# Softmax of two attentions: maxima subtracted by VectorE, one exponential of 512 columns in place of four with a bias

## Chip, core and metric

The kernel runs on one core of a Trainium2 chip. The metric is the device time of one execution in microseconds. Engines are named as in the profile: PE is TensorE (PEld its weight loads), DVE is VectorE, ACT is ScalarE, POOL is GpSimd, SP is SyncE.

## What is computed

A chain of layers on 16 sequences of 128 tokens and 256 channels. Two of them, the second layer's "ffn" (phase l1f) and the fourth layer's cross attention (phase l3x), hold a softmax attention of 16 heads of 16 channels, and both go through the same helper in the kernel. Cut to what matters:

```python
def _L1_ffn_ref(x, W_gate, W_qkv):            # phase l1f
    gating = jax.nn.softmax(x @ W_gate.T, axis=-1)
    ...
    att = jnp.einsum('bhqd,bkd->bhqk', q, k_shared) * (1.0 / math.sqrt(hd))
    att = jnp.where(causal[None, None, :, :], att, -jnp.inf)
    att = jax.nn.softmax(att, axis=-1)
    y = jnp.einsum('bhqk,bkd->bhqd', att, v_shared)
    ...
def _L3_xattn_ref(x, cond, mask, ...):        # phase l3x
    q = _w8a8_linear(x, wq, bq).reshape(B, N, H, D).transpose(0, 2, 1, 3)
    ...
    scores = jnp.einsum('bhnd,bhld->bhnl', q, k) * inv_sqrt_d + mask[:, None]
    attn = jax.nn.softmax(scores, axis=-1)
    o = jnp.einsum('bhnl,bhld->bhnd', attn, v)
    ...
    return _w8a8_linear(o, wo, bo)
```

Each row of each head's 128x128 scores has its maximum taken off, is put through exp, multiplied with the values and divided by its sum.

## The kernel before

The program is a sequence of phases with a barrier behind each. Every phase treats the 16 sequences ("blocks") one after the other, in a software pipeline. The list `order` gives the steps of a turn with their lags: in turn t, step (name, lag) works on block t - lag. Every engine walks the same list and does its own part of each step, so the list is also the order in each engine's queue. In phase l1f:

```python
order = (("S0", 2), ("P3", 3), ("stats", 0), ("V2", 3), ("qkv", 1),
         ("S1", 2), ("P0", 2), ("V3", 3), ("oT", 3), ("pick", 1), ("rows", 1),
         ("S2", 2), ("P1", 2), ("V0", 2), ("turn", 1), ("back", 3), ("normalise", 0), ("ternary", 0),
         ("S3", 2), ("P2", 2), ("V1", 2), ("xT", 0), ("divide", 3))
```

Class `HeadSoftmax` does the 16 heads in four groups of four heads, s = 0 to 3; a group's scores fill one PSUM bank, 128x512 f32. There are two banks `pS`, two tiles `ex` for the exponentials, two tiles `exT` for the transposed ones, and one bank `pP` for the transposes.

- Step S of group s. PE: `scores`, a matmul that writes the mask and one that adds q times k. DVE: `maximum` (line 1226), the negated maximum of each of the four heads, `negmax`. ACT: `exp` (line 1201), four activations of 128 columns each, with the head's `negmax` as bias.
- Step P. PE: `turn` (line 1167), four transposes of `ex` into `pP`. Then the evacuation of `pP` to `exT`: by ACT for groups 0 and 3 (line 1220), by DVE for groups 1 and 2 (line 1232).
- Step V. PE: `values` (line 1175), four matmuls with the values into `pO`. After the fourth group ACT copies `pO` to `oT` (line 1209), PE turns it back, and DVE divides by the sums (lines 1246, 1248).

What is interleaved differs. In l1f DVE also has "pick" (lines 1348 to 1354) and "rows" (lines 1358 to 1367, it makes the queries, the shared key `k_rows` and the values of the next block), the layer norm (`stats` lines 150 and 152, `xn` line 167) and a "ternary" step on weights of a later phase (lines 556 to 561). PE has "qkv" (line 895), the transposes "turn" of queries and keys (lines 866, 869), which ACT copies out (lines 877, 883), and "xT" (line 178, copied out by ACT in line 184). In l3x DVE quantises x and the attention's output (lines 1611 to 1626); PE turns the quantised x ("xq", line 1468), ACT copies it out (xqT, line 1509) and then copies the last two strips of kT ("spread", line 883); PE's next S0 waits for these. Its mask is f32 and comes by DMA.

`after(engine, semaphore, v)` waits until the semaphore has reached v, and is left out where v is a constant that is not positive. `hold` waits and then increments a spare semaphore, so that the instruction behind it starts only when the wait is met.

Of the kernel before, what the change touches and what calls it, by code (L numbers as in the profile page):

```python
# [13 lines left out]
ALU = mybir.AluOpType  # L14
ACT = mybir.ActivationFunctionType
AX = mybir.AxisListType
# [5 lines left out]
B, P, C = 16, 128, 256  # L22
# [8 lines left out]
def bc(ap, n):  # L31

    return ap.unsqueeze(2).to_broadcast([ap.shape[0], ap.shape[1], n])
# [6 lines left out]
class Chain:  # L40


    def __init__(self, eng, sem, per):
        self.eng, self.sem, self.per, self.base, self.n = eng, sem, per, None, per
# [42 lines left out]
def hold(eng, sem, v, spare):  # L87

    eng.wait_ge(sem, v)
    eng.sem_inc(spare, 1)  # L90


def after(eng, sem, v):

    if not (isinstance(v, int) and v <= 0):
        eng.wait_ge(sem, v)
# [802 lines left out]
def phase_l1_attention(nc, D, G):  # L899
# [7 lines left out]
    with Phase(nc, "l1x") as ph:  # L907
# [64 lines left out]
        def _(pe):  # L972
# [58 lines left out]
            for s in range(4):  # L1031
                steps[f"S{s}"] = lambda b, p, s=s: scores(b, p, s)
                steps[f"V{s}"] = lambda b, p, s=s: values(b, p, s)
            pipeline(pe, order, steps, peel=6)

        @block.scalar
        def _(act):
            def exp(b, p, s):
                act.wait_ge(clipped, 4 * b + s + 1)
                after(act, pv_done, 4 * b + s - 1)  # L1040
                act.activation(ex[s % 2][:].rearrange("p m t -> p (m t)"), sc[s % 2][:],
                               ACT.Exp).then_inc(exp_done, 1)

            def turn_out(b, p):
                act.wait_ge(attT_ps, b + 1)
                after(act, out_ps, b)
                act.activation(attT[:].rearrange("p k t -> p (k t)"), pT[:, C:2 * C],
                               ACT.Copy).then_inc(attT_ready, 1)

            def o_turned(b, p):  # L1050
                act.wait_ge(pv_done, 4 * b + 4)
                after(act, back_ps, b)
                act.activation(oT[:], pO[:], ACT.Copy).then_inc(oT_ready, 1)

            steps = {"xT": lambda b, p: nm.scalar(act, b, p), "turn": lambda b, p: tq.scalar(act, b, p),
                     "spread": lambda b, p: tq.scalar_rest(act, b, p), "attT": turn_out, "oT": o_turned}
            for s in range(4):
                steps[f"S{s}"] = lambda b, p, s=s: exp(b, p, s)
            pipeline(act, order, steps, peel=6)
# [73 lines left out]
class HeadSoftmax:  # L1133
# [7 lines left out]
    def __init__(self, ph, G, tq, pS, pP, pO, pB, mask_id, mask_of, v_of, k_of):  # L1141
        self.G, self.tq, self.pS, self.pP, self.pO, self.pB = G, tq, pS, pP, pO, pB
        self.mask_id, self.mask_of, self.v_of, self.k_of = mask_id, mask_of, v_of, k_of
        (self.sc_ps, self.max_ready, self.exp_done, self.pT_ps, self.pT_ready, self.pv_done, self.oT_ready, self.back_ps,
         self.norm_steps, self.normalised) = (
            ph.sem(n) for n in ("sc_ps", "max_ready", "exp_done", "pT_ps", "pT_ready", "pv_done", "oT_ready", "back_ps",
                                "norm_steps", "normalised"))
        self.oT = ph.sb("oT", [P, 4 * P])
        self.negmax = [ph.sb(f"negmax{i}", [P, 4]) for i in range(2)]
        self.ex = [ph.sb(f"ex{i}", [P, 4, P]) for i in range(2)]  # L1150
        self.exT = [ph.sb(f"exT{i}", [P, 4, P]) for i in range(2)]
        self.rec = ph.sb("rec", [P, NH])

    def scores(self, pe, b, p, s):
        if s == 0:
            pe.wait_ge(self.tq.ready, b + 1)
        after(pe, self.exp_done, 4 * b + s - 1)
        bank = self.pS[s % 2]
        pe.matmul(bank[:], lhsT=self.mask_id[:], rhs=self.mask_of(p), start=True, stop=True)
        pe.matmul(bank[:], lhsT=self.tq.plain[p][:, s, :], rhs=self.k_of(p, s).rearrange("p h t -> p (h t)"),  # L1160
                  start=False, stop=True, skip_group_check=True).then_inc(self.sc_ps, 1)
# [33 lines left out]
        return steps  # L1195

    def exp(self, act, b, p, s):
        act.wait_ge(self.max_ready, 4 * b + s + 1)
        after(act, self.pT_ps, 4 * b + s - 1)
        for m in range(4):  # L1200
            ins = act.activation(self.ex[s % 2][:, m, :], self.pS[s % 2][:, m * P:(m + 1) * P], ACT.Exp,  # L1201
                                 bias=self.negmax[s % 2][:, m:m + 1])
        ins.then_inc(self.exp_done, 1)

    def o_turned(self, act, b):

# [15 lines left out]

    def maximum(self, dve, b, p, s):
        dve.wait_ge(self.sc_ps, 4 * b + s + 1)
        after(dve, self.exp_done, 4 * b + s - 1)
        dve.tensor_reduce(self.negmax[s % 2][:], self.pS[s % 2][:].rearrange("p (m t) -> p m t", m=4), AX.X,  # L1226
                          ALU.max, negate=True).then_inc(self.max_ready, 1)

    def evacuate(self, dve, b, p, s):
        dve.wait_ge(self.pT_ps, 4 * b + s + 1)  # L1230
# [399 lines left out]
def phase_l2_attention(nc, D, G):  # L1630
# [12 lines left out]
    with Phase(nc, "l2x") as ph:  # L1643
# [67 lines left out]
        def _(pe):  # L1711
# [87 lines left out]

            def slot(b, p, g, last):  # L1800
                scores(b, p, g)
                if at_least(b, g, 1):
                    turn_probs(*before(b, p, g, 1))
# [705 lines left out]
```

## Time and profile before

| | us |
|---|---|
| median of 3 runs | 3066.3 |
| lowest and highest | 3066.07, 3066.52 |
| the profiled execution | 3068.69 |
| its span, first to last instruction | 3066.9 |
| phase l1f, first S0 to its end | about 1128 to 1376 of the span |
| phase l3x | about 2355 to 2640 of the span |

The profile is one execution. Its page gives the busy time of each engine; a windows view gives the same for chosen stretches, with the granted clock of PE (1.00 is full speed); a timeline lists the instructions in order of time, with the idle time of their engine before them and what ended it. An instruction's duration is not what it costs its engine: neighbours on one engine overlap where they do not depend on each other.

### The profile page before, as it was taken

The numbers are of one execution on the slowest core, as the hardware profiler recorded it, in microseconds if no ns is written. First come the engines' busy times: TensorE is split into PE (matmuls) and PEld (weight loads), VectorE is DVE, ScalarE is ACT, GpSimd is POOL, SyncE is SP. The second block draws the span as 40 slices with busy tenths as digits, with TensorE's granted clock in tenths as the row PEclk, the third lists the DMA queues.
The fourth block names the chain that finished last, engine by engine and source line by source line (L and its number), as shares of the span: only waits on it lengthen the run. The fifth ranks groups of instructions, "written<-read, shape, count | busy, mean of one in ns | idle before, by whom it ended". The sixth has DMA issues, their size and how long they took to land. (4 is left out here: it accounts for less than half of the span.)

```text
span 3066.9 us, 38953 instructions
## 1 busy us (share of the span) xinstructions
PE 2516.7 (82%) x11114; PEld 1545.9 (50%) x11141; DVE 1472.6 (48%) x3480; ACT 1064.3 (35%) x3193; POOL 583.8 (19%) x888
## 2 busy tenths in 40 slices
PE   2476799999978868878999999996444888689998
PEld 1223477667745534434666666664222554446665
DVE  3496311111135557765666666665775666521111
ACT  1002122222225535544555555553222555311111
POOL 1242122222212310003333333331000000101110
PEclk9996899999989979999999999998666999689999
DMA  2400000000030000000000000002000000000000
GB/s 78 186 0 1 8 6 8 5 5 5 5 124 1 0 2 1 0 6 1 1 0 0 0 0 0 0 0 98 0 0 3 4 3 4 0 1 0 0 0 27
DMA packets 20673, 44.76 MB, mean 15 GB/s; under 512 B 3712, under 2 KB 16384, under 8 KB 19200
## 3 DMA queue, kind: packets, MB, share of 16 engines
q1 hardware_dynamic: 20608, 43.98, 4.0%
q8 instruction: 31, 0.51, 0.1%
q14 instruction: 34, 0.28, 0.0%
HBM read 41.87 MB, written 2.10 MB: 14 GB/s over the span
## 5 line engine op out<-in xcount | busy, mean ns | idle before, releaser
L717 DVE TENSOR_TENSOR moe_hid<-moe_act_g,moe_pU 128x384 f32<-128x384 f32 x128 | 70.9, 554 | 444.2 <-ACT moe_act_g L689 444.2
L689 ACT ACTIVATE moe_act_g<-moe_pG 128x384 f32<-128x384 f32 x128 | 62.8, 490 | 425.3 <-PE moe_pU L644 425.3
L644 PE MATMUL moe_pG<-big,moe_xT 128*128 128x384 f32 x512 | 187.5, 489 | 4.1 <-POOL moe_xT L611 4.1
L1867 ACT ACTIVATE l2x_prob<-l2x_pS,l2x_nb,l2x_rms_q 128x256 f32<-128x256 f32 x256 | 142.4, 565 | 133.3 <-DVE l2x_nb L2015 133.3
L623 POOL TENSOR_TENSOR moe_hidw<-moe_hid,moe_data_w_all 128x384 f32<-128x384 f32 x128 | 105.8, 826 | 427.4 <-DVE moe_hid L717 420.7
L644 PE MATMUL moe_pU<-big,moe_xT 128*128 128x384 f32 x512 | 187.1, 488 | 0.0
L665 PE MATMUL moe_pO<-big,moe_hT 128*128 128x256 f32 x768 | 186.8, 380 | 0.0
L895 PE MATMUL l2x_pQ<-big,l2x_xT 128*128 128x512 f32 x320 | 154.6, 606 | 13.6 <-POOL l2x_cT L1944 10.9
L665 PEld LDWEIGHTS moe_pO<-big,moe_hT 128*128 128x128 f32 x768 | 136.0, 190 | 13.2
L689 ACT ACTIVATE l3f_act_g<-l3f_pG 128x512 f32<-128x512 f32 x64 | 38.2, 597 | 286.9 <-PE l3f_pU L644 286.9
L2012 DVE TENSOR_REDUCE l2x_negmax<-l2x_pS 128x2 f32<-128x512 f32 x128 | 87.7, 685 | 98.3 <-PE l2x_pS L1756 95.4
L644 PE MATMUL l3f_pG<-big,l3f_xT 128*128 128x512 f32 x256 | 122.2, 600 | 12.7 <-POOL l3f_xT L611 12.7
L644 PEld LDWEIGHTS moe_pU<-big,moe_xT 128*128 128x128 f32 x512 | 97.9, 191 | 68.5 <-issue 1.2
L1756 PE MATMUL l2x_pS<-l2x_kT,l2x_qT 128*128 128x256 f32 x512 | 128.3, 380 | 0.0
L1848 ACT ACTIVATE l2x_square<-l2x_pQ 128x128 f32<-128x128 f32 x384 | 101.7, 292 | 62.4 <-PE l2x_pQ L895 62.4
L1776 PE MATMUL l2x_pT<-big,l2x_oT 128*128 128x256 f32 x512 | 121.1, 379 | 0.7 <-ACT l2x_oT L1875 0.7
L644 PE MATMUL l3f_pU<-big,l3f_xT 128*128 128x512 f32 x256 | 121.5, 597 | 0.0
L644 PEld LDWEIGHTS moe_pG<-big,moe_xT 128*128 128x128 f32 x512 | 97.7, 191 | 46.2 <-issue 5.9
L665 PE MATMUL l3f_pO<-big,l3f_hT 128*128 128x256 f32 x512 | 120.9, 379 | 0.0
L1767 PE MATMUL l2x_pOT<-l2x_probT,l2x_v 128*128 128x512 f32 x256 | 120.4, 592 | 0.0
L1776 PEld LDWEIGHTS l2x_pT<-big,l2x_oT 128*128 128x128 f32 x512 | 97.0, 190 | 40.2 <-issue 28.7
L1201 ACT ACTIVATE l3x_ex<-l3x_pS,l3x_negmax 128x128 f32<-128x128 f32 x256 | 73.0, 368 | 127.1 <-DVE l3x_negmax L1226 122.2
(421 smaller groups left out, 5309.6 us busy)
## 6 DMA issues: line engine op xcount, KB each, us to landing
big<-in_e_gate SPq DMA_DIRECT2D x1, 3072.0 KB, 10.5
big<-in_e_up SPq DMA_DIRECT2D x1, 3072.0 KB, 17.4
big<-in_e_down SPq DMA_DIRECT2D x1, 3072.0 KB, 24.3
moe_lanes<-in_l2f_lanes SPq DMA_DIRECT2D x16, 192.0 KB, 2.8
x_all<-in_x SPq DMA_DIRECT2D x1, 2048.0 KB, 8.1
hyA_ctx<-in_ctx SPq DMA_DIRECT2D x16, 128.0 KB, 2.0
hyena_toep_rev<-in_k_rev SPq DMA_DIRECT2D x1, 2048.0 KB, 8.4
big<-in_l_wq SPq DMA_DIRECT2D x1, 2048.0 KB, 7.7
```

The source lines that it names most:

```text
L623: pool.tensor_tensor(hidw[c % 2][:].rearrange("p (e i) -> p e i", e=n), hid[c % 2][:].rearrange("p (e i) -> p e i", e=n), bc(w, chunk // n ...
L644: last = pe.matmul(ps[:, 0:chunk], lhsT=xT[p][:, k, :], rhs=w(k, c), start=(k == 0), stop=(k == KC - 1))
L665: last = pe.matmul(pO[p][:, 0:C], lhsT=hT[c % 2][:, k, :], rhs=w_down(c * KT + k), start=(c == 0 and k == 0), stop=(c == NC - 1 and k == K ...
L689: act.activation(act_g[c % 2][:], pG[c % 2][:, 0:chunk], ACT.Silu).then_inc(silu_done, 1)
L895: last = pe.matmul(out, lhsT=xT[:, k, :], rhs=w[:, k, cols], start=(k == 0), stop=(k == KC - 1))
L1201: ins = act.activation(self.ex[s % 2][:, m, :], self.pS[s % 2][:, m * P:(m + 1) * P], ACT.Exp, bias=self.negmax[s % 2][:, m:m + 1])
L1756: last = pe.matmul(pS[j][:, h * 2 * P:(h + 1) * 2 * P], lhsT=qT[g % 2][:, 2 * j + h, :], rhs=kT[p][:, g, :, :].rearrange("p a k -> p (a k) ...
L1767: last = pe.matmul(pOT[:], lhsT=v[p][:, a, g * P:(g + 1) * P], rhs=probT[:, a, :, :].rearrange("p h t -> p (h t)"), start=(a == 0), stop=( ...
L1776: last = pe.matmul(pT[:, C:2 * C], lhsT=oT[:, h, :], rhs=W["l2_wo"][:, 4 * g + h, :], start=(h == 0), stop=(h == 3))
L1848: ins = act.activation(square[u % 2][:, h, :], pQ[:, h * P:(h + 1) * P], ACT.Square, accum_out=ssq[u % 2][:, h:h + 1])
L1867: ins = act.activation(prob[g % 2][:, h, :], pS[j][:, (h % 2) * 2 * P:(h % 2 + 1) * 2 * P], ACT.Exp, scale=rms_q[g][:, h:h + 1], bias=nb[: ...
L2012: dve.tensor_reduce(negmax[:, c], pS[j][:].rearrange("p (h k) -> p h k", h=2), AX.X, ALU.max, negate=True).then_inc(S["max_steps"], 1)
```

## The change

DVE takes the maximum without negating it (`top`), waits until PE has transposed what stood in the tile `ex` two groups before, waits for its own reduce, and subtracts the broadcast maxima from the bank in one tensor_tensor of 128x512, writing to `ex` in SBUF. A new semaphore `shifted` tells of it. ACT then takes one exponential of all 512 columns, in place in `ex`, with no bias. PE's scores, which overwrite a bank, wait for the subtraction of two groups before in place of the exponential.

```diff
-        self.negmax = [ph.sb(f"negmax{i}", [P, 4]) for i in range(2)]
+        self.shifted = ph.sem("shifted")
+        self.top = [ph.sb(f"top{i}", [P, 4]) for i in range(2)]
...
     def scores(self, pe, b, p, s):
...
-        after(pe, self.exp_done, 4 * b + s - 1)
+        after(pe, self.shifted, 4 * b + s - 1)
...
     def exp(self, act, b, p, s):
-        act.wait_ge(self.max_ready, 4 * b + s + 1)
-        after(act, self.pT_ps, 4 * b + s - 1)
-        for m in range(4):
-            ins = act.activation(self.ex[s % 2][:, m, :], self.pS[s % 2][:, m * P:(m + 1) * P], ACT.Exp,
-                                 bias=self.negmax[s % 2][:, m:m + 1])
-        ins.then_inc(self.exp_done, 1)
+        act.wait_ge(self.shifted, 4 * b + s + 1)
+        flat = self.ex[s % 2][:].rearrange("p m t -> p (m t)")
+        act.activation(flat, flat, ACT.Exp).then_inc(self.exp_done, 1)
...
     def maximum(self, dve, b, p, s):
         dve.wait_ge(self.sc_ps, 4 * b + s + 1)
-        after(dve, self.exp_done, 4 * b + s - 1)
-        dve.tensor_reduce(self.negmax[s % 2][:], self.pS[s % 2][:].rearrange("p (m t) -> p m t", m=4), AX.X,
-                          ALU.max, negate=True).then_inc(self.max_ready, 1)
+        scores = self.pS[s % 2][:].rearrange("p (m t) -> p m t", m=4)
+        dve.tensor_reduce(self.top[s % 2][:], scores, AX.X, ALU.max).then_inc(self.max_ready, 1)
+        after(dve, self.pT_ps, 4 * b + s - 1)
+        hold(dve, self.max_ready, 4 * b + s + 1, self.G["spare"])
+        dve.tensor_tensor(self.ex[s % 2][:], scores, bc(self.top[s % 2][:], P), ALU.subtract).then_inc(self.shifted, 1)
```

On DVE in phase l1f, from the end of "rows" over the step S of group 2 to the layer norm (`vs` holds the values, `xn` the normalised x; - before, + with the change):

```order
 L1364 TENSOR_TENSOR l1f_picked<-l1f_pV,l1f_val 128x256
 L1367 TENSOR_REDUCE l1f_vs<-l1f_picked 128x16
-L1226 TENSOR_REDUCE l1f_negmax<-l1f_pS 128x4
+L1224 TENSOR_REDUCE l1f_top<-l1f_pS 128x4
+L1227 TENSOR_TENSOR l1f_ex<-l1f_pS,l1f_top 128x512
 L1232 COPY l1f_exT<-l1f_pP 128x512
 L167 TENSOR_SCALAR l1f_xn<-x_all,l1f_ln_mv,l1f_ln_rstd 128x256
```

The subtraction stands between the reduce and the evacuation of P1; nothing else changes place.

On ACT in phase l3x, from the step "aq" (the quantised attention output) to "spread", over the exponential of group 3:

```order
 L1514 ACTIVATE l3x_aqT<-l3x_pT 128x256
 L877 ACTIVATE l3x_qT<-l3x_pTq 128x512
 L883 ACTIVATE l3x_kT<-l3x_pTk 32x4x128 x2
-L1201 ACTIVATE l3x_ex<-l3x_pS,l3x_negmax 128x128 x4
+L1201 ACTIVATE l3x_ex<-l3x_ex 128x512
 L1509 ACTIVATE l3x_xqT<-l3x_pT 128x256
 L883 ACTIVATE l3x_kT<-l3x_pTk 32x4x128 x2
```

Four activations become one, and the order stays. On DVE in phase l3x, around the step S of group 3, between the quantised x (`qx_q`) and the division of an earlier block (`rec`, `att`), in a turn ahead of the loop:

```order
 L1621 TENSOR_SCALAR l3x_qx_y<-l3x_xn,l3x_qx_inv 128x256
 L1626 TENSOR_SCALAR l3x_qx_q<-l3x_qx_y 128x256
-L1226 TENSOR_REDUCE l3x_negmax<-l3x_pS 128x4
+L1224 TENSOR_REDUCE l3x_top<-l3x_pS 128x4
+L1227 TENSOR_TENSOR l3x_ex<-l3x_pS,l3x_top 128x512
 L1232 COPY l3x_exT<-l3x_pP 128x512
 L1246 RECIPROCAL l3x_rec<-l3x_pQK 128x16
 L1248 TENSOR_TENSOR l3x_att<-l3x_pQK,l3x_rec 128x256
```

Here too one instruction comes in behind the reduce.

## Rows read from the trace of the kernel before

**Rows 1.** The page's head and first section: busy us, share, instructions.
```profile
span 3066.9 us, 38953 instructions
PE 2516.7 (82%) x11114; PEld 1545.9 (50%) x11141; DVE 1472.6 (48%) x3480; ACT 1064.3 (35%) x3193; POOL 583.8 (19%) x888
```

**Rows 2.** Windows of one block each, two of l1f, one of l3x; first the columns.
```profile
core 0: us, PE busy (x) PEld busy (x) DVE busy (x) ACT busy (x) POOL busy (x), PEclk, DMA share, GB/s
1243.20:1258.05 14.85, 13.03 (x81) 6.67 (x80) 10.96 (x29) 7.95 (x27) 0.74 (x2) 1.00 0.00 0
1258.05:1272.78 14.73, 12.66 (x79) 6.74 (x80) 10.88 (x30) 7.96 (x27) 0.74 (x2) 1.00 0.00 0
2481.99:2498.94 16.95, 14.82 (x94) 8.55 (x93) 11.87 (x31) 9.24 (x26) 1.21 (x3) 1.00 0.01 4
```

**Rows 3.** Waits in the l1f block from 1243.20: who for whom, us, times, longest.
```profile
ACT l1f_ex L1201 <- DVE l1f_negmax L1226: 6.9, 4, 2.6
DVE l1f_negmax L1226 <- PE l1f_pS L1160: 2.6, 1, 2.6
```

**Rows 4.** Timeline of l1f, start and duration in us, in brackets idle time before.
```profile
1255.26 0.17 DVE L1342 TENSOR_REDUCE l1f_one<-l1f_pV 128x1 f32<-128x16 f32 x1 [0.25 <-PE l1f_pV L895]
...
1258.05 0.69 DVE L1226 TENSOR_REDUCE l1f_negmax<-l1f_pS 128x4 f32<-128x512 f32 x1 [2.62 <-PE l1f_pS L1160]
...
1262.02 0.65 PE L866 MATMUL l1f_pTq<-ident,l1f_q_rows 128*128 128x128 f32 x4 [0.48 <-DVE l1f_k_rows L1362]
...
1262.83 0.68 DVE L1226 TENSOR_REDUCE l1f_negmax<-l1f_pS 128x4 f32<-128x512 f32 x1
...
1263.43 0.68 DVE L1232 COPY l1f_exT<-l1f_pP 128x512 f32<-128x512 f32 x1
...
1265.91 0.68 DVE L1226 TENSOR_REDUCE l1f_negmax<-l1f_pS 128x4 f32<-128x512 f32 x1
...
1266.62 1.14 ACT L1201 ACTIVATE l1f_ex<-l1f_pS,l1f_negmax 128x128 f32<-128x128 f32 x4 [0.51 <-DVE l1f_negmax L1226]
...
1267.82 0.66 PE L1167 MATMUL l1f_pP<-ident,l1f_ex 128*128 128x128 f32 x4
...
1272.78 0.69 DVE L1226 TENSOR_REDUCE l1f_negmax<-l1f_pS 128x4 f32<-128x512 f32 x1 [2.62 <-PE l1f_pS L1160]
```

**Rows 5.** Groups of instructions kept apart by shape, busy us and mean ns; one timeline row.
```profile
L717 DVE TENSOR_TENSOR l3f_hid<-l3f_act_g,l3f_pU 128x512 f32<-128x512 f32 x32 | 22.0, 687 | 155.5 <-ACT l3f_act_g L689 155.5
L1226 DVE TENSOR_REDUCE l1f_negmax<-l1f_pS 128x4 f32<-128x512 f32 x64 | 43.8, 685 | 49.2 <-PE l1f_pS L1160 48.4 <-issue 0.6
L559 DVE TENSOR_SCALAR l1f_ternary_tmp<-l1f_ternary_tmp 128x384 f32<-128x384 f32 x16 | 5.8, 359 | 0.6
L1041 ACT ACTIVATE l1x_ex<-l1x_sc 128x512 f32<-128x512 f32 x64 | 40.3, 630 | 86.3 <-DVE l1x_sc L1095 59.8 <-PE l1x_pO L1004 25.8
L689 ACT ACTIVATE l3f_act_g<-l3f_pG 128x512 f32<-128x512 f32 x64 | 38.2, 597 | 286.9 <-PE l3f_pU L644 286.9
...
1269.55 0.18 DVE L152 BATCH_NORM_AGGREGATE l1f_ln_mv<-l1f_ln_stats 128x2 f32<-128x6 f32 x1 [0.16 <-DVE l1f_ln_stats L150]
```

**Rows 6.** Timeline of l3x, one block.
```profile
2485.69 0.69 DVE L1226 TENSOR_REDUCE l3x_negmax<-l3x_pS 128x4 f32<-128x512 f32 x1 [0.83 <-PE l3x_pS L1160]
...
2489.26 0.69 DVE L1226 TENSOR_REDUCE l3x_negmax<-l3x_pS 128x4 f32<-128x512 f32 x1 [0.77 <-PE l3x_pS L1160]
...
2493.36 0.69 DVE L1226 TENSOR_REDUCE l3x_negmax<-l3x_pS 128x4 f32<-128x512 f32 x1 [0.85 <-PE l3x_pS L1160]
...
2494.08 1.14 ACT L1201 ACTIVATE l3x_ex<-l3x_pS,l3x_negmax 128x128 f32<-128x128 f32 x4 [1.17 <-DVE l3x_negmax L1226]
...
2495.09 0.40 ACT L1509 ACTIVATE l3x_xqT<-l3x_pT 128x256 bf16<-128x256 bf16 x1
...
2495.64 0.38 PE L895 MATMUL l3x_pT<-l3x_woT,l3x_aqT 128*128 128x256 bf16 x2 [1.31 <-ACT l3x_xqT L1509]
...
2496.84 1.12 PE L1159 MATMUL l3x_pS<-l3x_mask,ident 128*128 128x512 f32 x2 [0.82 <-ACT l3x_kT L883]
```

**Rows 7.** Windows of two later blocks of l3x, columns as in rows 2.
```profile
2498.94:2517.80 18.86, 16.62 (x93) 9.18 (x92) 12.06 (x30) 9.24 (x26) 1.09 (x3) 0.88 0.01 3
2517.80:2537.57 19.77, 17.64 (x95) 9.83 (x94) 11.88 (x31) 9.24 (x26) 1.22 (x3) 0.86 0.01 3
```

## The prediction

> **What bounds the kernel now.** I start with the page [rows 1]: PE is busy 82% of the span, DVE 48%, ACT 35%. By those shares DVE has plenty of room, but they are averages over nine phases, and the change touches only two, l1f and l3x. So next come the windows, one block of each phase at a time [rows 2]. A block of l1f takes 14.85 or 14.73 us, PE busy 12.66 to 13.03, DVE 10.9, ACT 8.0. A block of l3x takes 16.95 us, PE 14.82, DVE 11.87, ACT 9.24. In neither is an engine full; what sets the period is a loop of dependences, to be followed in the timeline.
>
> In **l1f** [rows 4] the loop reads: DVE's reduce of S1 starts at 1258.05, that of S2 at 1262.83, that of S3 at 1265.91. Between them DVE carries no idle time: pick, rows, the evacuation of P1, xn and the ternary step stand there back to back (the list of waits of a block names DVE only before S1 [rows 3]). The exponential of S3 starts at 1266.62, and PE's P3 at 1267.82, as that ends. Then PE works through V2, the projections (qkv) and the scores of S1 without a gap until DVE can start the next S1 at 1272.78. The pieces: 7.86 us of DVE in a row, 1.91 from the reduce of S3 to P3, 4.96 of PE: 14.73, the period. DVE's only long idle stretch, 2.6 us a block [rows 3, 4], lies in the PE part of the loop, before S1. So in l1f each DVE microsecond between S1 and S3 is on the path though DVE is 74% busy; ACT is on it once a block, with the exponential of S3.
>
> In **l3x** [rows 6] DVE waits for PE's scores before each reduce (0.83, 0.77 and 0.85 us before S1, S2 and S3), while PE runs without a gap up to the transposes of x. There the loop leaves PE: reduce of S3 at 2493.36, exponential at 2494.08, then in ACT's order xqT at 2495.09 and the last two strips of kT, and PE's next S0 at 2496.84. PE waits 1.31 us for the first and 0.82 us for the second. So the path holds one reduce and one exponential a block.
>
> **The change part by part.** *The new subtraction.* A tensor_tensor of 128x512 f32 with one operand in PSUM stands in the trace: 687 ns [rows 5]. The broadcast of four maxima over 128 columns is the only difference. I take 0.69 us. It depends on the reduce just ahead of it; the same construction (a wait on DVE's own semaphore, held by an increment) in the statistics leaves 0.16 us idle, where independent neighbours overlap: S2's reduce to the copy behind it is 0.60 us from start to start at a duration of 0.68 [rows 4, 5]. So one group costs DVE 0.69 + 0.15 = 0.84 us more from start to start, 3.4 us a block, 64 groups in each phase. Bounds: below, 0.45 + 0.03 = 0.48, if it ran at the rate of the tensor_scalar from SBUF (359 ns for 384 columns [rows 5], 0.45 for 512) and the wait cost as little as 0.03; above, 1.0, with twice the wait. I take 0.84, since the row of the same instruction is the nearest.
>
> *The exponential.* Four of 128 columns take 1.14 us together [rows 4], one of 512 from SBUF to SBUF in l1x 630 ns [rows 5]: 0.51 us less, in each of 128 groups. Reading SBUF instead of the bank costs ACT something: 597 ns is the row with a PSUM source [rows 5], 33 ns apart.
> The Trainium skill (page "VectorE: DVE Perf Modes", section on the TRN2 errata) gives ScalarE a larger fixed cost for an SBUF source than for PSUM, 224 against 172 cycles; an estimate from these is 43 ns. That speaks against the change, the trace agrees in size, and by the page's figure the sum below would be about 0.3 us longer (29 exponentials on the path, 10 ns each).
>
> *The step from scores to finished exponential.* Before, on S3 of l1f: 1.91 us from the reduce to P3 [rows 4]. After: 0.69 + 0.15 + 0.69 + 0.03 + 0.63 + 0.06 = 2.25. So **+0.33 us** where DVE has waited for scores; where groups queue up on DVE, +0.84 for each.
>
> *The bank.* PE's scores wait for the subtraction two groups back instead of the exponential. PE's own order has the transposes of that group ahead, and they wait for its exponential, so this wait is met already, before and after: 0. Likewise DVE's new wait for the transposes of group s-2 (their tile is overwritten): PE did them before the scores that DVE has just waited for: 0. Behind the subtraction on DVE are queued the pick and rows chain (S1), the evacuation of P1 (S2) and P2 (S3), and PE's turn, P2 and P3 wait for these.
>
> *Sum for l1f.* S1 and S2 lengthen DVE's stretch by 0.84 each, and S3's step grows by 0.33: +2.01 us a block. Everything else on the loop's way I shift by the same rows: PE's turn, already waiting 0.48 for k_rows [rows 4], comes 0.84 later, P2 some 1.2 later, xT some 1.2 later, and P3 2.0 later. It is P3 that closes the loop, as before. P2's evacuation on DVE ends about when the exponential of S3 does, at no extra cost. DVE's own work is then 14.73 - 2.62 - 0.25 (its wait for pV) + 3.36 = 15.2 us [rows 4], under the new period of 16.75: it idles 1.5 before S1. There are 16 blocks (64 reduces, four a block [rows 5]), 14 periods from the S1 of the first to that of the fifteenth: 28.1. In the last two blocks DVE waits for scores again; up to 8 steps of 0.33 there: 2.6. **l1f: +30.7 us.**
>
> *Sum for l3x.* The exponential of S3 starts 0.84 later, and xqT behind it starts 0.53 after it instead of 1.01 (one instruction less its overlap with the next): +0.36 a block on both PE waits, 15 periods: 5.4. DVE's slack of 0.77 to 0.85 before S1 to S3 is just used up by 0.84 each; what is missing, under 0.1 in every second block, gives 0.7. The tail, where PE waits for single exponentials, about 3 times 0.33: 1. **l3x: +7.1 us.** The cover here is thin: each further 0.1 us of a subtraction would put about 0.2 a block on the path, 3 us in all.
>
> Nothing else moves: the other phases run the same instructions, and POOL and SP have no part in the groups. The profiled execution took 3068.69 (span 3066.9), the median is 3066.3; the difference of 37.8 goes onto the median. **Forecast: 3066.3 + 30.7 + 7.1 = 3104.1, so 3104 us.**
>
> **Rivals.** *A, the clock falls more often (14%).* In l3x PE waits twice within 2.6 us each block, and in two blocks running the granted clock was 0.88 and 0.86 instead of 1.00, so part of them ran at 1.2 in place of 2.4 GHz; they took 18.86 and 19.77 us against some 17.0 [rows 2, 7], 2.3 us more each. The change stretches these waits to 1.67 and 0.85, and in l1f puts waits of near 1 us before the turn and P3, with PE's share down from 86% to 77%. Against it: l1f shows 1.00 in the blocks of [rows 2] with waits of 0.5 us, and l3x mostly 1.00 with 1.31. If five more blocks fall: +12, 3116; if every one of the 15 periods did: 13 more at 2.3, +30, 3134.
> [...]
>
> *B, the subtraction is cheap (5%).* At the lower bound of 0.45 us with a 0.15 wait, l1f gains 2 x 0.60 + 0.09 a block, 18 us plus 1 in the tail, and l3x about 2: 3087. Against it: both f32 tensor_tensor rows run at one column per ns.
>
> *C, DVE's idle time hides it (4%).* DVE idles 3.9 us a block in l1f, and the four groups need 3.4. Were these idle pieces spread between S1 and S3, only the latency of +0.33 in l3x would remain: 3072, within 0.2%. The timeline speaks against it, since 2.62 of the 3.9 lie in one piece behind PE.
>
> *D, faster (3%).* Were ACT's queue what PE waits for, the shorter exponential would pay: in l3x 0.48 a block on xqT, in l1f 0.51 on P3, together 15 x 0.48 + 16 x 0.51 = 15.4, so 3051. PE's waits do name ACT (1.31, 0.82). It needs the subtraction to cost nothing on the path: it decides below 0.48 us from start to start in l3x, and below 0.17 in l1f (0.51 over three groups). The nearest row says 0.84.
>
> **How the numbers follow.** My forecast holds 72% (3097 to 3112, with the self-wait between 0.05 and 0.25 us and the two slow blocks there or gone, -4.7), A 14%, B 5%, C 4%, D 3%; 2% is for what I have not seen. From 3091 to 3121 takes the forecast, the first half of A and the upper edge of B: 8 in 10 or somewhat more. 0.2% is 6 us, about what a measurement of this kernel can tell from no change. Slower by more than that: forecast, A, B and part of the rest, 0.94; within it: C, 0.03; faster: D, 0.03.
>
> **What would show each step.** In the profile after: the subtraction at 0.69 with 0.15 idle before it, the exponential at 0.63; a block of l1f at 16.75 with DVE without a gap from S1 to S3, P3 released by ACT or DVE, and DVE's wait before S1 down from 2.62 to 1.5; a block of l3x at 17.3 with DVE's waits before S1 to S3 near 0, and PE's wait for xqT at 1.67. I am wrong if the l1f block stays below 16, if l3x grows by more than 1 us a block at a clock of 1.00, or if the clock rows fall in l1f.

## The result and the profile after

The changed kernel takes 3136.0 us (3133.9 to 3137.9 over four runs), the kernel before beside it on the same chip 3066.4. The ratio is 1.0226, 95% interval 1.0209 to 1.0244: slower by 69.6 us. I had forecast 3104, in a range from 3091 to 3121. The direction was right; the size lies outside the range.

The page's head and first section, changed kernel (busy us, share of the span, instructions; compare [rows 1]):

```profile
span 3136.1 us, 38599 instructions
PE 2553.2 (81%) x11114; PEld 1564.9 (50%) x11141; DVE 1559.3 (50%) x3608; ACT 1005.7 (32%) x2809; POOL 585.4 (19%) x888
```

DVE has 86.7 us more, for 128 new instructions, ACT 58.6 less, as meant. But PE, whose instructions are the same in number (11114), is busy 36.5 us longer. The same work took PE longer, and the granted clock is where to look.

The two new instructions by form, busy us and mean ns, then idle time before them:

```profile
L1227 DVE TENSOR_TENSOR l1f_ex<-l1f_pS,l1f_top 128x512 f32<-128x512 f32 x64 | 44.3, 692 | 9.1
L1201 ACT ACTIVATE l1f_ex<-l1f_ex 128x512 f32<-128x512 f32 x64 | 40.3, 630 | 167.9 <-DVE l1f_ex L1227 167.9
```

**l1f.** Two blocks, windows from S1 to S1, then the waits of the first of them (columns as in [rows 2, 3]):

```profile
core 0: us, PE busy (x) PEld busy (x) DVE busy (x) ACT busy (x) POOL busy (x), PEclk, DMA share, GB/s
1290.83:1307.74 16.91, 13.00 (x81) 6.67 (x80) 13.68 (x33) 6.06 (x15) 0.74 (x2) 1.00 0.00 0
1307.74:1324.46 16.72, 12.60 (x79) 6.74 (x80) 13.57 (x33) 6.06 (x15) 0.74 (x2) 1.00 0.00 0
```

```profile
ACT l1f_ex L1201 <- DVE l1f_ex L1227: 10.7, 4, 3.9
DVE l1f_top L1224 <- PE l1f_pS L1161: 1.6, 1, 1.6
```

The timeline of that block, cut to the loop (start, duration, in brackets idle time before), answers to [rows 4]:

```profile
1290.83 0.69 DVE L1224 TENSOR_REDUCE l1f_top<-l1f_pS 128x4 f32<-128x512 f32 x1 [1.59 <-PE l1f_pS L1161]
1291.66 0.69 DVE L1227 TENSOR_TENSOR l1f_ex<-l1f_pS,l1f_top 128x512 f32<-128x512 f32 x1
1292.27 0.16 DVE L1348 TENSOR_REDUCE l1f_val<-l1f_g 128x1 f32<-128x16 f32 x1
...
1300.27 0.68 DVE L1224 TENSOR_REDUCE l1f_top<-l1f_pS 128x4 f32<-128x512 f32 x1
1301.10 0.69 DVE L1227 TENSOR_TENSOR l1f_ex<-l1f_pS,l1f_top 128x512 f32<-128x512 f32 x1
...
1301.82 0.63 ACT L1201 ACTIVATE l1f_ex<-l1f_ex 128x512 f32<-128x512 f32 x1 [1.81 <-DVE l1f_ex L1227]
...
1302.79 0.66 PE L1168 MATMUL l1f_pP<-ident,l1f_ex 128*128 128x128 f32 x4 [0.92 <-ACT l1f_ex L1201]
...
1307.74 0.69 DVE L1224 TENSOR_REDUCE l1f_top<-l1f_pS 128x4 f32<-128x512 f32 x1 [1.72 <-PE l1f_pS L1161]
```

This is the picture that was forecast. The subtraction starts 0.83 us after its reduce. From the reduce of S1 to that of S3 it is 9.44 us in place of 7.86, from there to P3 2.52 (2.26 in the next block) in place of 1.91, and PE's part up to the next S1 is 4.95, as before. DVE's idle time before S1 shrank from 2.62 to 1.59. Fourteen periods grew from 206.4 to 234.6 us, and the phase ended 31.3 us later (1369.2 to 1400.5; the table of times before puts its end too late, at about 1376).

**l3x.** Five blocks in a row, windows from S0 to S0; compare 16.95 at a clock of 1.00 in [rows 2] and the two of [rows 7]:

```profile
2514.33:2534.68 20.35, 17.65 (x94) 9.78 (x93) 14.75 (x35) 7.46 (x14) 1.09 (x3) 0.84 0.01 3
2534.68:2554.58 19.90, 17.31 (x94) 9.75 (x93) 14.57 (x34) 7.46 (x14) 1.22 (x3) 0.86 0.01 3
2554.58:2572.96 18.38, 15.68 (x94) 8.78 (x93) 14.66 (x35) 7.46 (x14) 1.09 (x3) 0.95 0.01 4
2572.96:2592.90 19.94, 17.35 (x94) 9.55 (x93) 14.56 (x34) 7.46 (x14) 1.22 (x3) 0.84 0.01 3
2592.90:2613.22 20.32, 17.61 (x94) 9.76 (x93) 14.75 (x34) 7.46 (x14) 1.09 (x3) 0.84 0.01 3
```

None of the 15 blocks runs at full clock; before, 12 of 15 did. The same matmuls keep PE busy 15.7 us in one block of four and 17.3 to 17.7 in the others, where it was 14.8. The 15 periods from the first S0 to the sixteenth grew from 258.0 to 292.8 us. The timeline of one block shows where in it the clock goes; it answers to [rows 6]:

```profile
2547.22 0.69 DVE L1224 TENSOR_REDUCE l3x_top<-l3x_pS 128x4 f32<-128x512 f32 x1
2548.06 0.69 DVE L1227 TENSOR_TENSOR l3x_ex<-l3x_pS,l3x_top 128x512 f32<-128x512 f32 x1
...
2548.79 0.63 ACT L1201 ACTIVATE l3x_ex<-l3x_ex 128x512 f32<-128x512 f32 x1 [1.64 <-DVE l3x_ex L1227]
2549.44 0.38 ACT L1509 ACTIVATE l3x_xqT<-l3x_pT 128x256 bf16<-128x256 bf16 x1
...
2549.97 0.38 PE L895 MATMUL l3x_pT<-l3x_woT,l3x_aqT 128*128 128x256 bf16 x2 [1.77 <-ACT l3x_xqT L1509]
...
2551.17 2.07 PE L1160 MATMUL l3x_pS<-l3x_mask,ident 128*128 128x512 f32 x2 [0.82 <-ACT l3x_kT L883]
```

PE now waits 1.77 us for xqT (1.31 before), then 0.82 for kT as before, and the mask's matmul behind these two waits takes 2.07 us instead of 1.12: it runs at 1.2 GHz in place of 2.4, and so do the ones behind it for a while.

The balance of the span's 69.2 us: 31.3 in l1f, 2.7 from there to l3x, 36.4 in l3x, and 1.2 less behind it. The stretch between the two phases holds the same instructions before and after; the 2.7 there was forecast as nothing, and its cause is open. So the l1f term was right, and the l3x term, 7.1, came out five times as large.

### The profile page after: what moved, and what is told of

It reads as the page before. It is cut to its first block and busy times, and to the rows that moved or that the text cites. A ratio compares the mean times of both kernels' runs of the same rounds, so it can differ in the third digit from the quotient of the medians.

```text
span 3136.1 us, 38599 instructions
## 1 busy us (share of the span) xinstructions
PE 2553.2 (81%) x11114; PEld 1564.9 (50%) x11141; DVE 1559.3 (50%) x3608; ACT 1005.7 (32%) x2809; POOL 585.4 (19%) x888
## 5 line engine op out<-in xcount | busy, mean ns | idle before, releaser
L1940 POOL TENSOR_TENSOR l2x_rows<-l2x_part 128x512 f32<-128x512 f32 x80 | 101.5, 1269 | 7.7 <-DVE l2x_part L1993 0.2
```

What stands on the lines that cost most here:

```text
L1940: pool.tensor_tensor(rows[u % 2][:], part[u % 2][0][:], part[u % 2][1][:], ALU.add).then_inc(S["add_done"], 1)
```

## Experiments

Two theories stand against each other. *Clock*: in l3x the change lengthens PE's wait for xqT from 1.31 to 1.77 us, and this makes the granted clock fall in nearly every block; the direct cost is the 7 us that were forecast. *DVE*: VectorE's extra 3.4 us a block has become the bound of l3x, and PE's lower clock is only seen because PE is slack.

**The change in one phase at a time.** A flag for each use of the helper keeps the old exponentials or takes the new way:

```diff
-                         lambda p, h: v[p][:, h, :], lambda p, m: tq.blocks[p][:, m, :, :])
+                         lambda p, h: v[p][:, h, :], lambda p, m: tq.blocks[p][:, m, :, :], subtract=False)
```

> The change made in l1f alone; l3x keeps the bias form. Theory (each DVE microsecond between S1 and S3 is on l1f's path, and the two phases are independent): l1f block 16.76 us as in the changed kernel, phase +31.3, l3x as before with at most a few slow blocks, in all 3066 + 31 + 2 = 3100 (3096 to 3106). Rival (part of the cost of l3x comes from the shift in time that l1f causes, since l3x starts 34 us later, which would move where its clock falls): l3x slow here too though unchanged, up to +25 more, 3125.

Measured: 3096.4 (3091.9 to 3099.2), ratio 1.0098, interval 1.0081 to 1.0115.

> The change made in l3x alone. Theory (the longer pause of PE behind the transposes of x, 1.77 us in place of 1.31, makes the clock fall in nearly every block): +36, 3102, mean block of l3x 19.5 us, granted clock near 0.86 in most blocks. Rival (the shift in time): l3x +7 to +12, 3075, clock 1.00 in most blocks.

Measured: 3101.8 (3098.2 to 3104.5), ratio 1.0112, interval 1.0095 to 1.0129. The 15 periods of l3x sum to 292.6 us, at clocks of 0.84 to 0.95.

The kernel before took 3064.8 beside both, so the parts cost 31.6 and 37.0, together 68.6 of the 69.6. They add up, and the clock in l3x falls whether or not l1f is changed.

**Work for PE in the gap.** The changed kernel, with one matmul of the identity with itself, 128x512 f32, into the bank that is free, behind the transposes of x. It computes nothing that is used; it fills PE's wait.

```diff
+                for _ in range(1):
+                    pe.matmul(pS[0][:, 0:4 * P], lhsT=G["ident"][:], rhs=G["ident"][:].unsqueeze(1).to_broadcast([P, 4, P]),
+                              start=True, stop=True)
```

> The changed kernel with one more matmul of 128x512 f32 on PE behind the transposes of x in l3x, into a score bank that is free then; its result is overwritten by the scores. It fills about 0.9 of the 1.77 us that PE waits there. Theory (the clock falls because PE pauses there): clock 1.00 in all l3x blocks, block 17.3 to 17.5, so l3x returns to about +7, in all 3136 - 28 = 3108 (3104 to 3114). Rival (the clock has nothing to do with this pause, or DVE is what lengthens the blocks): block still 19.5, 3136 or somewhat more.

Measured: 3107.7 (3104.6 to 3110.7), ratio 1.0138, interval 1.0121 to 1.0155. Windows of three blocks in l3x:

```profile
2498.01:2515.50 17.49, 15.72 (x96) 8.80 (x95) 14.65 (x34) 7.46 (x14) 1.09 (x3) 1.00 0.01 4
2515.50:2532.91 17.41, 15.74 (x96) 8.81 (x95) 14.56 (x35) 7.46 (x14) 1.22 (x3) 1.00 0.01 4
2532.91:2551.74 18.83, 17.04 (x96) 9.22 (x95) 14.64 (x35) 7.46 (x14) 1.09 (x3) 0.93 0.01 3
```

Giving PE *more* to do made the kernel 28 us faster than the changed one. That refutes the DVE theory: DVE does the same 14.6 us a block here, and the block takes 17.4. But every fourth block still fell (18.96, 18.83 and 18.71). Seven of the 15 stood below a clock of 1.00: these three, the one behind each (0.98 or 0.99) and the first (0.90). The time met the expectation, but that part of it was wrong: the theory wanted 1.00 in all. So a second dose was tried at the end, two matmuls of 384 columns:

> The changed kernel with more filler on TensorE in l3x: two matmuls of 384 columns into the free bank behind the transposes of x, in place of one of 512. With the one of 512 TensorE's wait for xqT went from 1.77 to 0.85 us, and every fourth block still fell (18.7 to 19.0 us at a clock of 0.92). Theory (the waits of TensorE in the long turn decide, and the other one of 0.8 to 0.9 us before S0 is not touched): with a wait of some 0.4 us left for xqT, as in the kernel before with the 512 columns (where none fell), all blocks run at 1.00 and take 17.4 to 17.5; four blocks gain 1.4 each, so 3107.7 - 5.6 = 3102 (3098 to 3105). Rival (the wait before S0 alone, 0.93 us in every second block, is what makes every fourth block fall): four blocks of 18.7 or more stay, 3107 or more.

Measured: 3101.9 (3099.3 to 3104.2), ratio 1.0110, interval 1.0093 to 1.0127. Two blocks, and PE's wait in one of them:

```profile
2500.62:2518.11 17.49, 16.15 (x98) 9.17 (x97) 14.66 (x35) 7.46 (x14) 1.09 (x3) 1.00 0.01 4
2518.11:2535.51 17.40, 16.16 (x98) 9.18 (x97) 14.56 (x34) 7.46 (x14) 1.22 (x3) 1.00 0.02 5
```

```profile
2514.78 0.38 PE L895 MATMUL l3x_pT<-l3x_woT,l3x_aqT 128*128 128x256 bf16 x2 [0.41 <-ACT l3x_xqT L1512]
2516.09 1.12 PE L1160 MATMUL l3x_pS<-l3x_mask,ident 128*128 128x512 f32 x2 [0.93 <-ACT l3x_kT L883]
```

All blocks at 1.00; the rival (the wait before S0 alone makes it fall) is refuted, since that wait of 0.93 is still there. This also measures the change's direct cost in l3x, free of the clock. The 15 periods take 259.5 us here and 252.2 in the kernel before with its gap filled (a run below), where all blocks are at 1.00 too: 7.3 us more. The other 33.3 (292.8 - 259.5) is the clock; the kernel before lost 5.8 to it in its three fallen blocks (258.0 - 252.2).

**The same wait without the change.** The kernel before, nothing on DVE, but copies on ACT ahead of xqT into scratch tiles, so that PE's wait grows:

```diff
+                act.activation(pad[0][p][:, 0:256], pTb[:, 0:256], ACT.Copy)
+                act.activation(pad[1][p][:, 0:64], pTb[:, 0:64], ACT.Copy)
                 act.activation(xqT[:].rearrange("p k t -> p (k t)"), pTb[:, 0:C], ACT.Copy).then_inc(xqT_ready, 1)
```

> The kernel before, untouched but for two more copies on ACT in l3x (256 and 64 columns, to scratch tiles) ahead of xqT, which delay xqT by about 0.46 us, as much as the change did. Nothing on DVE. Theory (the pause alone makes the clock fall): PE's pause before the out projection 1.77, clock falls in most l3x blocks, l3x about +35, 3101 (3094 to 3106). Rival (DVE's subtractions, which use up DVE's slack, make l3x slow): only 15 x 0.46 = +7, 3073.

Measured: 3091.1 (3081.2 to 3096.1), ratio 1.0071, interval 1.0045 to 1.0096. The wait was 1.70 us, and two blocks looked like this, with DVE's work as before the change (12 us):

```profile
2494.20:2514.15 19.95, 17.43 (x94) 9.63 (x93) 11.88 (x31) 9.63 (x28) 1.22 (x3) 0.84 0.01 3
2514.15:2534.47 20.32, 17.69 (x94) 9.84 (x93) 12.06 (x31) 9.63 (x28) 1.09 (x3) 0.84 0.01 3
```

The mechanism is shown: l3x lost 27.5 us to 0.39 us more of waiting for xqT, of which the wait itself is some 6 (15 x 0.39). The size was 10 us short of what I had expected, and outside the range that I had given. The profile is of one of the two longer executions, 3095.8; the other two took 3081.2 and 3086.4. Smaller doses, the copy of 64 columns alone and the one of 256 alone:

> The kernel before, with one copy of 64 columns on ACT in l3x ahead of xqT, which delays xqT by about 0.15 us (pause 1.46; it was 1.31 before and 1.77 in the change, where 2 and 15 blocks had the lower clock). Theory (the number of slow blocks grows with the pause): 4 to 8 blocks of l3x below 1.00, +2 for the copies and 2.3 for each further slow block, 3066 + 2 + 9 = 3077 (3068 to 3086). Rival (a step: nothing until some length of pause): 2 slow blocks, 3068.

Measured: 3065.0 (3063.6 to 3069.8), ratio 1.0004, interval 0.9994 to 1.0013. A miss of mine: I had expected an effect that grows with the wait. PE waited 1.43 us, blocks took 17.06 and 17.18 (0.11 more), and after the first none fell in the profiled execution.

> The kernel before with one copy of 256 columns on ScalarE ahead of xqT in l3x, nothing on VectorE: a dose between the copy of 64 columns (TensorE's wait 1.42 us, no block slowed by it, 3065) and the two copies (1.77 us, nearly all blocks slow, 3091). TensorE's wait should be 1.60 to 1.70, a block at full clock 17.3, 3070 if none falls. Theory of a step: it lies between 1.42 and 1.77, and on its upper side nearly all blocks fall at once: either near 3070 with at most three slow blocks, or near 3086 with ten or more. Rival (a gradual effect): about half of the blocks slow, near 3078.

Measured: 3083.0 (3081.4 to 3089.0), ratio 1.0053, interval 1.0035 to 1.0071. Four blocks in a row:

```profile
2453.32:2473.19 19.87, 17.46 (x94) 9.68 (x93) 11.88 (x30) 9.54 (x27) 1.22 (x3) 0.84 0.01 3
2473.19:2493.13 19.94, 17.42 (x95) 9.82 (x94) 12.07 (x31) 9.54 (x27) 1.09 (x3) 0.86 0.01 3
2493.13:2510.36 17.23, 14.82 (x94) 8.55 (x93) 11.87 (x30) 9.54 (x27) 1.21 (x3) 1.00 0.01 4
2510.36:2528.48 18.12, 15.60 (x93) 8.72 (x92) 12.07 (x31) 9.54 (x27) 1.09 (x3) 0.95 0.01 4
```

A wait of 1.59 us, and the same four repeat to the end of the phase: one at 1.00, one at 0.95, two near 0.85. The time lies between the two expectations, the number of blocks that fell (11 of 15) on the side of the step. But the profile is of the slowest of the four executions, 3089.0; the other three took 3081.4 to 3083.2, some 6 us less. If that difference lies in l3x, it is about 3 fallen blocks at 2.2 us each (33.3 over 15 in the changed kernel), which leaves an estimate of 8 in those. So the step is steep, but not shown to be sharp. By dose, from the profiled executions, with the blocks that fell below a clock of 1.00 among 15:

| kernel | wait for xqT, us | fallen | 15 periods, us |
|---|---|---|---|
| before | 1.31 | 3 | 258.0 |
| one copy of 64 | 1.43 | 1 | 254.9 |
| one copy of 256 | 1.59 | 11 | 278.2 |
| both copies | 1.70 | 14 | 285.5 |
| the change | 1.77 | 15 | 292.8 |

So between 1.43 and 1.59 us in this loop the fallen blocks went from one to most (about half, by that estimate, in the faster executions); the kernel before stood 0.1 to 0.3 us from there. The change pushed it over with 0.46.

**Filling the gap before the change.** The filler of 512 columns in the kernel before asks what the rare slow blocks cost there:

> The kernel before, with one more matmul of 128x512 f32 on PE in l3x behind the transposes of x, overwritten by the scores. Theory: the two blocks of l3x in which the clock fell run at 1.00, blocks 16.95 to 17.1, -4.6: 3061. Rival (the matmul is itself in the way, the pause being short): +0.2 a block, 3069.

Measured: 3061.3 (3059.4 to 3065.2), ratio 0.9989, interval 0.9980 to 0.9999, all blocks at 1.00, PE's wait 0.40. The gain is about 4 us, as expected.

**Taking the wait away.** ACT alone walks another order in l3x, with xqT and the last strips of kT ahead of group 3's exponential:

```diff
+            early = [o for o in order if o[0] not in ("spread", "xq")]
+            at = [o[0] for o in early].index("S3")
+            early[at:at] = [("spread", 1), ("xq", 0)]
-            pipeline(act, order, {**sm.scalar_steps(act), "xq": turn_x, "aq": turn_a,
+            pipeline(act, early, {**sm.scalar_steps(act), "xq": turn_x, "aq": turn_a,
```

> The kernel before with ACT's order alone changed in l3x: the last two strips of kT and xqT stand ahead of the exponential of S3 instead of behind it. Theory (PE's pause of 1.31 + 0.82 us stands behind that exponential): xqT right behind the transposes of x, pause near 0.4 in all, block 15.3 us, no slow block, l3x -30, 3036 (3030 to 3045). Rival (the exponential of S3, now later, holds P3, and PE waits there instead): block 16.5 or more, 3058.

Measured: 3039.5 (3037.0 to 3041.7), ratio 0.9919, interval 0.9902 to 0.9935. PE's wait for xqT and one block of l3x:

```profile
2464.41 0.38 PE L895 MATMUL l3x_pT<-l3x_woT,l3x_aqT 128*128 128x256 bf16 x2 [0.56 <-ACT l3x_xqT L1509]
```

```profile
2436.20:2452.00 15.80, 14.69 (x92) 8.55 (x92) 11.86 (x32) 9.26 (x26) 1.22 (x3) 1.00 0.02 5
```

This beats both kernels. The exponential of S3 was on the loop only because of its place in ACT's queue. The same order in the changed kernel:

> The changed kernel with one thing more: in l3x ScalarE copies out xqT and the last strips of kT ahead of group 3's exponential, as in the run that reordered the kernel before. This asks what the change costs in l3x when TensorE no longer waits a long time in one piece. Theory (the slow blocks come from that one wait of 1.77 us): TensorE's wait for xqT is near 0.6, the clock stays near 1.00, and VectorE sets the period: 12.65 us of its work in a block of the reordered kernel (15.5 less 2.9 idle) plus 3.4 for the subtractions is 16.0, at most 16.3, so l3x takes 240 to 245 where the reordered kernel took 228.6; with 34 from l1f and l2x, 3039.5 + 34 + 14 = 3087 (3080 to 3095). Rival (it is TensorE's lower share of busy time that costs the clock, not the one long wait): the blocks take 17.5 to 19 at a clock under 0.95, the time is 3110 or more.

Measured: 3076.1 (3073.8 to 3079.2), ratio 1.0035, interval 1.0020 to 1.0050. Two blocks of l3x:

```profile
2482.94:2498.96 16.02, 15.14 (x100) 8.52 (x92) 14.38 (x35) 7.35 (x14) 1.09 (x3) 1.00 0.01 4
2498.96:2514.97 16.01, 14.90 (x92) 8.53 (x92) 14.26 (x35) 7.34 (x14) 1.22 (x3) 1.00 0.01 4
```

The clock stays at 1.00 in every block, as the clock theory says, and a steady block takes the 16.0 expected. PE is busy for 93 to 95% of these blocks, so the run doesn't tell its theory (the long wait) from its rival (PE's share of busy time). The sum, though, is 234.6 us, 6.0 above the reordered kernel before, where I had expected 14: I had priced all 15 periods as steady ones, and the first four take only 13.1 to 16.0. The whole change costs 36.6 us on top of this order, 29 of it ahead of l3x.

**DVE's queue in l1f.** The changed kernel with the ternary step moved from between S2 and S3 to ahead of S1, into DVE's idle time:

```diff
-        order = (("S0", 2), ("P3", 3), ("stats", 0), ("V2", 3), ("qkv", 1),
+        order = (("S0", 2), ("P3", 3), ("stats", 0), ("V2", 3), ("qkv", 1), ("ternary", 0),
                  ("S1", 2), ("P0", 2), ("V3", 3), ("oT", 3), ("pick", 1), ("rows", 1),
-                 ("S2", 2), ("P1", 2), ("V0", 2), ("turn", 1), ("back", 3), ("normalise", 0), ("ternary", 0),
+                 ("S2", 2), ("P1", 2), ("V0", 2), ("turn", 1), ("back", 3), ("normalise", 0),
```

> The changed kernel with the ternary step of l1f (1.46 us of DVE) moved from between S2 and S3 into DVE's idle stretch before S1 (1.6 us). Theory (DVE between S1 and S3 is on the path, DVE before S1 is not): the exponential of S3 comes 1.46 earlier, but P3 then waits for PE's own S0, 0.9 earlier: l1f block 15.9 instead of 16.76, -13, 3123. Rival (DVE's total work sets the block): unchanged, 3136.

Measured: 3123.6 (3122.8 to 3124.7), ratio 1.0192, interval 1.0175 to 1.0209; blocks of 15.57 and 15.77, every third 16.0 to 16.4. Those five are the ones in which the clock fell, as the second of these two shows:

```profile
1234.38:1249.94 15.56, 12.62 (x81) 6.81 (x80) 13.63 (x33) 6.06 (x15) 1.28 (x2) 1.00 0.00 0
1249.94:1266.38 16.44, 14.20 (x81) 7.71 (x80) 13.85 (x33) 6.07 (x15) 0.95 (x2) 0.90 0.00 0
```

The same DVE work in another place gave back 12.4 us, so the l1f term is place, not amount. For the kernel before, with the layer norm's last step moved too, on top of ACT's order in l3x:

> The kernel before, exponentials with a bias and no subtraction, with two orders changed: ScalarE's in l3x as above, and in l1f the layer norm's last step and the ternary step moved from between the reduces of groups 2 and 3 to ahead of group 1's, where VectorE idles 2.62 us a block. Theory (in l1f each microsecond of VectorE between group 1 and group 3 is on the path, its idle time ahead of group 1 is not): some 1.3 us of VectorE's 7.86 leave the path, TensorE comes next as the bound at 13.0 to 13.3 us of work a block, so a block of l1f goes from 14.73 to 13.5 or 13.8, 14 periods give 13 to 17 us: 3039.5 - 15 = 3024 (3021 to 3028). Rival (the clock falls in l1f as VectorE's order shifts the waits, or another wait takes the place): the l1f block stays above 14.4, 3035 or more.

Measured: 3037.0 (3035.4 to 3038.6), ratio 0.9906, interval 0.9888 to 0.9924. A miss: blocks went from 14.73 only to 14.38 and 14.60, and the 15 periods gave 4 us, not 15. DVE's waits in the loop show why:

```profile
1246.24 0.69 DVE L1226 TENSOR_REDUCE l1f_negmax<-l1f_pS 128x4 f32<-128x512 f32 x1 [0.65 <-PE l1f_pS L1160]
1249.61 0.69 DVE L1226 TENSOR_REDUCE l1f_negmax<-l1f_pS 128x4 f32<-128x512 f32 x1 [0.74 <-PE l1f_pS L1160]
...
1254.22 0.69 DVE L1226 TENSOR_REDUCE l1f_negmax<-l1f_pS 128x4 f32<-128x512 f32 x1 [0.69 <-PE l1f_pS L1160]
```

DVE now waits for PE's scores before each of these groups, and PE for its operands three times a block (0.56 for exT, 0.48 for k_rows, 0.43 for kT). Another loop had stood 0.35 us behind the first. The intervals of this kernel and of the reordered one overlap; both are about 0.9% below the kernel before.

## Why the prediction was wrong in size

- **Price of the subtraction: right.** 0.69 us by the row of the same form; 692 ns measured. Start 0.83 to 0.84 after the reduce; 0.84 forecast. The exponential took 630 ns, as forecast. Two slips beside it don't touch the sum: 359 ns for 384 columns is 0.48 us for 512, not 0.45, and [rows 5] show one f32 tensor_tensor and not two, at 687 ns for 512 columns or 1.34 ns a column.
- **The step from S3 to P3: about right.** +0.33 forecast; 2.26 to 2.52 in place of 1.91, so +0.35 to +0.61. In the block shown P3 starts 0.41 us after the end of P2's evacuation and 0.34 after the exponential; I had said that the evacuation costs nothing extra. Which of the two held it isn't settled; it is 0.1 us a block on average, and DVE's stretch was 0.1 shorter than forecast.
- **l1f: right.** 16.75 a block forecast, 16.72 and 16.91 measured; 30.7 forecast, 31.3 measured, 31.6 alone. DVE's wait before S1 1.59 to 1.72, forecast 1.5. The moved ternary step shows that the reason was right too. But a sign that I had named for being wrong did come: the clock rows fell in l1f, 7 of 15 blocks at 0.87 or 0.90, none before (5 to 7 in each of the six profiles of kernels with the change in l1f). In the first 14 periods it cost nothing, 234.6 us with the fallen ones in different places. It cost about 1 us in the last, 13.44 at 0.87 against 12.48 at 1.00 in the kernel with l1f alone changed.
- **l3x, the direct part: about right.** 17.3 a block forecast, 17.4 to 17.5 at full clock; PE's wait 1.67 forecast, 1.77 measured, since xqT starts 0.65 us after the exponential (2548.79 to 2549.44) and not 0.53. Over the 15 periods 7.3 at full clock against 6.1 (5.4 + 0.7).
- **l3x, the clock: the step that failed.** It was rival A, "the clock falls more often", with the price it named: "if every one of the 15 periods did", 3134, and 3136 was measured. I gave it 14%, and my range held only its first half. The fault is in its "against it": "l3x mostly 1.00 with 1.31". I read the many blocks at 1.00 as a margin. Two blocks in a row at 0.88 and 0.86 in the same steady loop [rows 7] spoke against that: the doses put the change from few to most blocks between 1.43 and 1.59 us, below the 1.67 that I had worked out for the changed loop. What the runs showed in its place: all 15 blocks fell, and the clock took 33.3 us of l3x where it had taken 5.8 before, 27.5 more. So the sum had 0 for a term of 27.5 us.
- The Trainium skill ("TensorE: Matmul & The Clock Gate", section "HAM oscillation") tells of a kernel whose PE waits for a DMA in each step, longer than the step's matmuls take, and loses its clock in each. The trace here shows the loss with far shorter waits: 1.77 and 0.82 us beside 14.8 of matmuls, and 15 of 15 blocks at 0.84 to 0.95. So that section did not settle this loop either way.
- **Rivals B, C and D** fell as argued: the subtraction cost its 0.84, nothing was hidden in DVE's idle time, and no gain appeared.

With its gap filled the changed kernel is 35.0 us above the kernel before beside it, and the kernel before with its gap filled is 3.7 below: 38.7 us for the change where no block of l3x falls, and the forecast was 37.8. What was missing was the clock in l3x.

## What to carry to other kernels

Here a loop in which a few blocks showed a lower granted clock had no margin. One loop is no rule, but where a trace shows such blocks I would now work out how much longer PE's longest wait becomes, and give "every block falls" a main chance, not a tail. Such a wait can be filled with matmuls that nobody uses (here 34 us), but it is better taken away by the order of the engine that PE waits for: here that was worth 26 us before the change and 60 after. Moving work from a slack engine to a slack engine is priced by the place in the queue where it lands; 0.84 us in the middle of DVE's unbroken stretch cost all of it, though DVE was idle 26% of the time.

## What was not expected of the hardware

- **The fall comes within a narrow band.** 1.43 us of waiting: 1 block of 15; 1.59 us: 11 of 15 in the slowest execution, and some 8, by the estimate above, in the others. A fallen block cost 2.2 us on average in the changed kernel.
- **It repeats every four blocks.** With the copy of 256 columns the clocks are 1.00, 0.95, 0.84, 0.86 and again; with the change 0.95, 0.84, 0.84, 0.86; with the filler of 512 columns one block of four is at 0.93. What makes four is open.
- **The wait's length alone doesn't decide.** The changed kernel with the filler of 512 columns waits 0.85 us for xqT and still loses one block in four; the kernel before waits 1.31 and rarely does. With the change a block is 0.4 us longer and PE's waits stand elsewhere in relation to the rest. PE's busy share of a block doesn't decide either: 75% in the changed kernel's l1f blocks at 1.00 (12.60 of 16.72), 87% in l3x before, where few fall (14.82 of 16.95), and 90% with the filler of 512 columns (15.74 of 17.41), where one in four does. The filler shortens the wait and raises the share at once. It multiplies identities, mostly zeros; other data was not tried. I can't tell these causes apart.
- **A lower clock may cost nothing.** The first l1f blocks of the changed kernel show 0.90, and PE is busy 13.91 us where it was 12.60, yet the block is as long, since DVE's stretch and not PE sets it:

```profile
1173.17:1189.88 16.71, 13.91 (x79) 7.56 (x80) 13.57 (x33) 6.06 (x15) 0.74 (x2) 0.90 0.00 1
```

With the ternary step moved, DVE's stretch is shorter, and the same fall lengthens the block: 15.56 us at 1.00, 16.44 at 0.90. PE's waits ahead of the fall in the block from 1173.17 are no longer than 1.00 us, so waits of l3x's length are not needed for one:

```profile
1175.98 0.63 PE L1168 MATMUL l1f_pP<-ident,l1f_ex 128*128 128x128 f32 x4 [0.88 <-ACT l1f_exT L1218]
...
1177.97 0.70 PE L866 MATMUL l1f_pTq<-ident,l1f_q_rows 128*128 128x128 f32 x4 [1.00 <-DVE l1f_k_rows L1362]
...
1178.96 1.09 PE L1186 MATMUL l1f_pQK<-ident,l1f_oT 128*128 128x128 f32 x4
```

At full clock the last of these takes 0.63 us.
